# New lists of steps for five engines of a hand-scheduled language model block

## The reference

```python
h = _L0_tok_ref(x, w0, w1)
h = h + _L0_attn_ref(_layernorm(h), ...)          # A, then B
q = _GRID[searchsorted(_MID, abs(xn))] * sign(xn) * scale   # FP4 in blocks of 16
h = h + fp4_linear(silu(gate) * y, w_down)         # C
```

## Time and profile before

| | |
|---|---|
| median of 3 runs | 774.72 us (774.24 to 775.47) |
| span of the profiled execution | 772.5 us |
| PE busy | 701.0 us (91%) |
| DVE busy | 591.7 us (77%) |
| ACT busy | 509.2 us (66%) |
| POOL busy | 144.3 us (19%) |
| chain that ended last | PE 74%, DVE 11%, ACT 9%, issue 4% |
| mean granted clock of PE | 0.964 |

### The profile page before, as it was taken

One profiled execution on the slowest core, in us unless ns is written; L12 is line 12 of the kernel. 1 busy time (PEld: TensorE's weight loads), 2 busy tenths in 40 slices (PEclk: granted clock), 3 DMA queues, 4 the chain that ended last, 5 costly groups with the idle time before them and its releaser, 6 DMA issues.

```text
span 772.5 us, 9862 instructions
## 1 busy us (share of the span) xinstructions
PE 701.0 (91%) x3301; PEld 563.6 (73%) x3301; DVE 591.7 (77%) x1023; ACT 509.2 (66%) x888; POOL 144.3 (19%) x220
## 2 busy tenths in 40 slices
PE   4465788899999999999999999999999999899676
PEld 3325656787788867886788777896888777788574
DVE  0678777888788879788778878887988878872763
ACT  2556796698568966597749866797749774861221
POOL 2403301430032302230142103230232003000000
PEclk9687899999999999999999999999999999899999
DMA  4800000000010000010010001000010000000000
GB/s 124 275 2 27 3 25 2 27 10 20 15 41 1 28 14 14 28 28 1 14 42 2 28 15 41 1 28 10 4 42 1 1 14 15 1 0 14 15 0 28
DMA packets 13374, 19.34 MB, mean 25 GB/s; under 512 B 982, under 2 KB 10764, under 8 KB 13324
## 3 DMA queue, kind: packets, MB, share of 16 engines
q1 hardware_dynamic: 10720, 10.31, 4.1%
q0 software_dynamic: 2560, 8.39, 3.7%
q10 hardware_dynamic: 44, 0.01, 0.0%
HBM read 14.51 MB, written 4.19 MB: 24 GB/s over the span
## 4 chain that ended last, share of the span: by engine, by line
PE 74%; DVE 11%; ACT 9%; issue 4%; DMA 1%; POOL 0%; ACTq 0%; DVEq 0%; POOLq 0%
PE psB L556 20%; PE psC L652 11%; PE psC L625 11%; PE psB L583 11%; PE psA L547 9%; PE psA L519 5%; PE psC L639 3%; PE psA L507 2%; ACT hT L745 1%; ACT mix L754 1%; DMA rows<-L_tok_w,ids_now 1%; DVE top L360 1%; ACT take L800 1%; PE psA L529 1%; PE psC L611 1%
## 5 line engine op out<-in xcount | busy, mean ns | idle before, releaser
L556 PE MATMUL psB<-cwv_s,kkT 128*128 128x256 f32 x512 | 113.9, 380 | 0.0
L556 PEld LDWEIGHTS psB<-cwv_s,kkT 128*128 128x128 f32 x512 | 96.2, 190 | 15.7 <-issue 3.3
L652 PE MATMUL psC<-downT,hqT 128*128 128x256 f32 (+1 forms) x384 | 96.7, 397 | 0.0
L625 PE MATMUL psC<-up_hi,xq_hi 128*128 128x352 f32 x256 | 88.2, 345 | 9.2 <-DVE xq_lo L1202 8.5
L547 PE MATMUL psA<-mix,kvr_s 128*128 128x512 f32 x192 | 88.6, 606 | 3.4 <-ACT vT L776 2.4
L652 PEld LDWEIGHTS psC<-downT,hqT 128*128 128x128 f32 (+1 forms) x384 | 69.4, 192 | 26.4 <-issue 19.0
L625 PE MATMUL psC<-up_hi,xq_lo 128*128 128x352 f32 x256 | 83.8, 327 | 0.0
L625 PE MATMUL psC<-up_lo,xq_hi 128*128 128x352 f32 x256 | 83.6, 327 | 0.0
L447 POOL TENSOR_SCALAR sc_c<-mv_c 128x2 f32<-128x2 f32 x16 | 7.0, 436 | 371.7 <-DVE mv_c L1134 371.7
L547 PEld LDWEIGHTS psA<-mix,kvr_s 128*128 128x128 f32 x192 | 36.5, 194 | 42.4 <-issue 39.3
L519 PE MATMUL psA<-w_s,rowsT 128*128 128x256 f32 x256 | 59.5, 386 | 0.0
(11 more groups left out here) (163 smaller groups left out, 1488.5 us busy)
## 6 DMA issues: line engine op xcount, KB each, us to landing
out<-h SPq DMA_DIRECT2D x16, 256.0 KB, 2.1
mix<-L_attn_cwk SPq DMA_DIRECT2D x1, 1024.0 KB, 8.0
cwv_s<-L_attn_cwv SPq DMA_DIRECT2D x1, 1024.0 KB, 10.9
kkT<-L_ffn_w_gate SPq DMA_DIRECT2D x1, 704.0 KB, 4.6
kkT<-L_ffn_w_up SPq DMA_DIRECT2D x1, 704.0 KB, 6.7
hqT<-L_ffn_w_down SPq DMA_DIRECT2D x1, 704.0 KB, 7.8
w_s<-L_tok_w SPq DMA_DIRECT2D x1, 512.0 KB, 3.9
rows<-L_tok_w,ids_now POOLq DMA_INDIRECT x32, 4.0
```

Source lines behind the costliest of these rows:

```text
L556: mm = nc.tensor.matmul(psB[:, B.slot(name), q * D:(q + 1) * D], lhsT[:, k, (2 * j + q) * P:(2 * j + q + 1) * P], weight[:, k, :], start=( ...
L625: mm = nc.tensor.matmul(psC[:, C.slot(name), f, 0:INTER // 2], a[:, k, t * P:(t + 1) * P], b[:, w, k, f * (INTER // 2):(f + 1) * (INTER // ...
L652: mm = nc.tensor.matmul(psC[:, C.slot(name), 0, q * D:(q + 1) * D], hqT[0:n, q, k, :], downT[0:n, k, :], start=(k == 0), stop=(k == KI - 1))
```

## The change

Only the table `ORDER` is written anew. No instruction, buffer or wait is added or taken away. Two lines show its form (before, after):

```diff
-        ("c_turn2", 3), ("a_r", 1), ("c_turn3", 3), ("b_value1", 2), ("a_turn0", 0), ("c_down1", 3), ("b_out0", 1),
+        ("b_key2", 2), ("a_k", 1), ("b_key3", 2), ("a_v", 1), ("c_down0", 3), ("b_value0", 2), ("c_turn2", 3),
+        ("w_turn2", 2), ("b_value1", 2), ("a_r", 1), ("c_turn3", 3), ("a_turn0", 0), ("c_down1", 3), ("b_out0", 1),
```

More of the change, by code:

```diff
@@ L66 @@
 ORDER = {
[5 rows of a table removed]
-    "act": [("c_cols1", 1), ("w_par", -3), ("b_cols", 0), ("b_part", 0), ("c_up1", 1), ("a_emb1", -1),
[7 rows of a table removed]
-    "dve": [("c_split1", 4), ("b_mix", 3), ("a_stat", 2), ("c_up1", 4), ("w_par", -3), ("b_low", 3), ("w_quant2", 3),
[5 rows of a table removed]
-        ("b_coef", -2)],
-    "sp": [("c_down1", 2), ("c_down0", 1)],
[5 rows of a table added]
+    "act": [("c_cols1", 1), ("b_cols", 0), ("b_part", 0), ("c_up1", 1), ("a_emb1", -1), ("w_par", -3),
[7 rows of a table added]
+    "dve": [("w_quant1", 3), ("c_split1", 4), ("b_mix", 3), ("c_up1", 4), ("a_stat", 2), ("b_low", 3),
[6 rows of a table added]
+        ("a_coef", -3)],
+    "sp": [("c_down0", 2), ("c_down1", 2)],
 }
```

## The result

The changed kernel takes 780.64 us (median of 4 runs, 780.07 to 781.67), the kernel before 774.55 (774.24 to 775.47) beside it: ratio 1.0077, 95% interval 1.0063 to 1.0091. The forecast was 776.1 us, in a range of 773.3 to 778.9. So it is slower by 6.1 us, where 1.4 were forecast. The profiled spans are 778.2 and 772.5.

A forecast was written before the change was run, and what follows sets the result against it. PE was taken to bound the full iterations (busy 84.04 of 84.50 us), with chains of waits through ACT and DVE in filling and draining. Full iterations 0, filling +0.7, draining +0.7 gave +1.4 on 774.72: 776.1 us, range 773.3 to 778.9.

The forecast's parts named there:

- Full iterations: The six iterations with all three parts, 154 to 661 us: 0 forecast, bounds -2.7 to +3.
- ACT and the remaining swaps of DVE: In the full iterations, the other reorderings on ACT and DVE: steps move 0.7 to 4 us inside slack, no cost.
- the ones of POOL: In the full iterations, POOL's swaps, counted among those that move steps inside slack, no cost.
- Rival A: A new PE wait in each full iteration, ahead of `a_k` or at `a_turn0`: +3, 779.1 us; chance 0.20.
- Filling: Pipeline start, chunks 0 and 1: +0.7, from +0.15 carried, +0.37 at chunk 1's end and +0.2 for the lower clock.
- Draining, last stage: Chunk 7's last stage: DVE finishes `b_value1` before `c_norm0`, so `c_norm1` starts 0.7 later, reaching the end; bounds 0 to 1.0.
- Draining, the stage ahead of it: The iteration with `b_out` of chunk 7: `c_up0` later on PE, but no loss, since `c_cols1` waits for DVE as before.
- A gain from `w_turn2`: Chunk 1's filling: its 1.6 us of PE and the 1.24 us wait leave the stretch between `b_out0` and `b_out1`.
- rival B: Faster: chunk 1's 3.3 us stretch goes in full, plus one PE wait per iteration, no draining loss: 773.0 us; chance 0.15.

The follow-up runs named there:

- e1: The changed kernel with POOL's list alone put back as it was before; 777.01 us, ratio 1.0026 to the kernel before.
- e4: The kernel before with POOL's list alone as in the changed kernel; 774.92 us, ratio 0.9999.
- e7: The kernel before with only PE's `w_turn2` moved, from behind `b_out0` to behind `c_turn2`; 772.92 us, ratio 0.9959.

## Why the prediction was wrong, by its own steps

- **Full iterations, the step that failed first.** "ACT and the remaining swaps of DVE", "the ones of POOL" among them, were said to "move steps of 0.7 to 4 us inside slack". That was worked out for PE, ACT and DVE; POOL's swap was not followed. Of a moved DMA its landing counts, and of the step behind it what else its queue holds. The term measured +3.0, where 0 was taken with +3 as its end. e1 shows that POOL's list, with the rest of the change, is its cause; e4 that the list needs the rest.
- Rival A had the sign and near the price (3 us), in another place and form: it was to be in each iteration or in none, and was 1.6 and 1.2 us in two and 0.1 or less in the others, because the landing time differs from one iteration to the next.
- The rest of this term was right: `c_cols0` had about 2.0 us of slack (2.1 worked out), and `c_norm1` started 6.75 us behind `b_out0` in the iterations from 396 us on (6.66 worked out); in the second, at 310.20, it was 7.10.
- **Filling: right in its working.** From `b_key3` of chunk 0 (107.69, before 108.29) to `b_out0` of chunk 1 (138.91, before 137.09) were 31.2 us instead of 28.8, +2.4 where 2.6 were worked out. ACT after, between the two copies of v:

```profile
114.51 0.60 ACT L777 ACTIVATE vT<-psA 128x512 f32<-128x512 f32 x1 [1.12 <-PE psA L548]
138.91 5.30 PE L557 MATMUL psB<-wo_s,rT 128*128 128x256 f32 x16 [1.88 <-DVE rT L995]
144.55 0.66 PE L612 MATMUL psC<-ident,normc 128*128 128x128 f32 x4 [0.34 <-DVE normc L377]
```

  `b_out` ran at the lower clock for its larger part: 5.30 us, and the granted clock was 0.50 in the window of 138 to 139 us and 0.64 in 140 to 143. `a_emb0` came 0.4 early (145.05) instead of 0.4 late. 1.3 us of it are chance: the first `b_gate` took 6.78 us in the profiled execution of before, at a granted clock of 0.53 between 90.0 and 93.1 us, and 5.36 to 5.55 us in all 19 other traces. Without it the filling is +0.9, and +0.7 was forecast.
- **Draining, last stage: right.** `c_norm1` of chunk 7 started at 728.05, 53.25 us behind `b_gate`, against 52.52 before (722.13): +0.73, with 0.7 forecast; to the end +0.5.
- **Draining, the stage ahead of it: the second step that failed.** "The iteration before it (`b_out` of chunk 7) loses nothing by my working: PE does `c_up0` later there, but the `c_cols1` behind it waits for the same chain of DVE as before." `c_norm1` did keep its distance from `b_out0` (6.75 against 6.80). But `c_up0` started 2.9 us later, behind a wait of 2.73 us, and ran at the lower clock for much of its length. Its 24 matmuls took 5.5 us where they had taken 3.9, and ended behind `c_norm1`: `c_cols1` came 12.4 us behind `b_out0` instead of 11.8. DVE's part of `c_up0`, which waits for it, came 0.9 later, PE waited 3.71 us in front of `c_up1`'s second half, and ran this too at the lower clock. Windows of after and of before (columns as in rows 1), then the first matmul of that second half, after and before:

```profile
657.00:662.00 5.00, 4.92 (x21) 4.92 (x22) 4.03 (x8) 2.88 (x4) 3.33 (x5) 0.66 0.00 0
651.50:655.40 3.90, 3.90 (x25) 3.81 (x24) 3.80 (x13) 0.31 (x1) 2.60 (x2) 1.00 0.00 0
670.54 0.43 PE L626 MATMUL psC<-up_hi,xq_hi 128*128 128x352 f32 x1 [3.71 <-DVE xq_lo L1203]
666.92 0.44 PE L625 MATMUL psC<-up_hi,xq_hi 128*128 128x352 f32 x1 [0.38 <-DVE xq_lo L1202]
```

  From these to `b_gate` are 4.26 us after (0.72 granted in 669 to 675 us) and 2.69 before (1.00 in 667 to 669.6), +1.57; with the 0.95 by which the second half started later that is the 2.5 us, with 0 taken. At its former pace `c_up0` would have ended at 661.0, ahead of `c_norm1`'s end at 661.97, and `c_cols1` would have come as before (my estimate from these rows). So the term failed for most of its size by the granted clock, which the prediction worked into the filling and left out here. The sum of the terms as measured is 3.0 + 2.6 + 0.5 - 0.4 = 5.7, the difference of the spans.
- A gain from `w_turn2`, which rival B counted on, is there in the timed runs of e7, without the rest; where it arises its trace does not show.
